# Attention and FFN layer: output projection as three fp32r passes, normalisation in PSUM, query rounded by ScalarE

## The reference

```
xn   = layernorm(x)
q    = xn @ Wq + bq                      16 heads of 16
k, v = ctx @ Wk + bk, ctx @ Wv + bv      one head, shared by all
attn = softmax(mask(q k^T / 4)) v        64 keys
x    = x + attn @ Wo + bo
h    = layernorm(x)
m    = mix0 * h[t-1] + mix1 * h[t] + mix2 * h[t+1]
s    = tanh(m @ Wo1 + bo1) @ Wo2 + bo2   a score for each of 9 paths
p    = argmax(s)
c    = (m @ W1[p] + b1[p]) @ W2[p] + b2[p]
out  = x + layernorm(h + c) * gamma + beta
```

## Time and profile before

| what | value |
|---|---|
| median of three runs | 359.27 us (357.69 to 359.3) |
| the profiled execution's own time | 357.65 us |
| its span | 355.8 us |
| PE busy | 312.0 us, 88% |
| DVE busy | 282.4 us, 79% |
| POOL busy | 188.2 us, 53% |
| ACT busy | 183.0 us, 51% |
| mean granted clock of PE | 0.973 of full speed |
| `project_out`'s matmuls (L584) | 128 records, mean 390 ns, 31.3 us |

### The profile page before, as it was taken

One profiled execution on the slowest core, in us unless ns is written; L12 is line 12 of the kernel. 1 busy time (PEld: TensorE's weight loads), 2 busy tenths in 40 slices (PEclk: granted clock), 3 DMA queues, 4 the chain that ended last, 5 costly groups with the idle time before them and its releaser, 6 DMA issues.

```text
span 355.8 us, 7313 instructions
## 1 busy us (share of the span) xinstructions
PE 312.0 (88%) x2700; PEld 230.7 (65%) x2700; DVE 282.4 (79%) x606; ACT 183.0 (51%) x285; POOL 188.2 (53%) x226
## 2 busy tenths in 40 slices
PE   1588788765999999999999999999999999799990
PEld 1374364452667957795678767876678568677980
DVE  2675398595769899889989898989798866689866
ACT  1452835625764477537851777258444752367400
POOL 0444002633178179944895299728881787164044
PEclk9998999996999999999999999999999999899996
DMA  7509500020002001200110010000100010001003
GB/s 210 177 0 218 106 0 1 2 76 0 0 4 76 0 2 62 73 3 0 59 52 22 0 59 0 0 0 2 61 0 2 2 61 2 0 0 62 3 0 118
DMA packets 20564, 13.44 MB, mean 38 GB/s; under 512 B 10097, under 2 KB 20282, under 8 KB 20538
## 3 DMA queue, kind: packets, MB, share of 16 engines
q1 hardware_dynamic: 18898, 12.53, 12.0%
q10 hardware_dynamic: 1640, 0.57, 0.7%
HBM read 8.90 MB, written 4.19 MB: 37 GB/s over the span
## 4 chain that ended last, share of the span: by engine, by line
PE 76%; DVE 12%; ACT 5%; issue 3%; POOL 2%; DMA 1%; DVEq 0%; ACTq 0%; POOLq 0%
PE ps L429 16%; PE ps L434 7%; PE ps L584 7%; PE ps L668 6%; PE ps L673 5%; PE ps L669 5%; PE ps L541 5%; PE ps L566 4%; PE ps L560 4%; DVE mx L1115 3%; DVE osb L1139 3%; PE ps L650 2%; PE ps L544 2%; PE ps L635 2%; PE ps L481 2%
## 5 line engine op out<-in xcount | busy, mean ns | idle before, releaser
L1408 POOL TENSOR_TENSOR rs<-ve,halfneg 128x4 f32<-128x4 f32 x24 | 26.7, 1113 | 106.8 <-DVE ve L1078 106.8
L843 ACT ACTIVATE e<-ps 128x1024 f32<-128x1024 f32 x32 | 31.1, 1024 | 20.3 <-PE ps L548 20.3
L1115 DVE TENSOR_REDUCE mx<-ps 128x16 f32<-128x1024 f32 x32 | 37.9, 1216 | 0.3 <-PE ps L516 0.3
L668 PE MATMUL ps<-w2h,hmh 128*128 128x256 f32 (+1 forms) x140 | 35.6, 288 | 0.0
L669 PE MATMUL ps<-w2l,hmh 128*128 128x256 f32 (+1 forms) x140 | 34.7, 283 | 0.0
L1465 POOL TENSOR_TENSOR hml<-hs,hmh 128x512 fp32r<-128x512 f32 x24 | 30.3, 1276 | 7.4 <-ACT hmh L904 7.3
L868 ACT ACTIVATE xh<-x,vb,rs 128x256 f32<-128x256 f32 x32 | 16.6, 591 | 33.5 <-POOL vb L1421 33.5
L584 PE MATMUL ps<-wo,osb 128*128 128x256 f32 x128 | 31.3, 390 | 2.0 <-DVE osb L1139 2.0
L894 ACT ACTIVATE hs<-ps,b1s 128x512 f32<-128x512 f32 x28 | 19.3, 689 | 24.4 <-PE ps L434 24.4
L1454 POOL TENSOR_TENSOR y<-xh2f,gms 128x256 f32<-128x256 f32 x28 | 22.2, 824 | 17.5 <-DVE xh2f L1087 17.5
L429 PE MATMUL ps<-xmh,w1h 128*128 128x512 f32 x80 | 27.8, 429 | 3.3 <-DVE xmh L1190 3.3
(11 more groups left out here) (161 smaller groups left out, 787.5 us busy)
## 6 DMA issues: line engine op xcount, KB each, us to landing
xin<-in_x SPq DMA_DIRECT2D x8, 512.0 KB, 4.1
out<-y SPq DMA_DIRECT2D x7, 512.0 KB, 2.9
min_<-in_mask_Bx1xSxS_ik SPq DMA_DIRECT2D x8, 128.0 KB, 4.8
hs<-in_L_ffn_W SPq DMA_DIRECT2D x2, 288.0 KB
y<-in_constants SPq DMA_DIRECT2D x1, 512.0 KB, 8.7
hs<-in_L_ffn_W SPq DMA_DIRECT2D x1, 512.0 KB
out<-xin SPq DMA_DIRECT2D x2, 256.0 KB, 2.2
cst<-in_constants SPq DMA_DIRECT2D x1, 384.0 KB, 6.0
```

The source lines that it names most:

```text
L668: nc.tensor.matmul(o, L.hi(m, r)[:, ks], w2h[0:r, m, :], start=(m == 0), stop=False)
L843: nc.scalar.activation(e[:, 2 * i:2 * i + 2, :], ps[:, bank:bank + 2, :], ACT.Exp).then_inc(s_e, 1)
L1115: v.tensor_reduce(mx[:, k, :].rearrange("p (a h) -> p a h", a=2), ps[:, bank:bank + 2, :].rearrange("p a (h s) -> p a h s", s=SK), AX.X, A ...
L1408: g.tensor_tensor(ln[7][:, :], ln[6][:, :], halfneg[:, :], ALU.pow).then_inc(s_r, 1)
```

## The change

Wo is split once into a rounded part `woh` (ACT) and a remainder `wol` (POOL), and PE's wait before the first step with an n is for `wol`. Wo is loaded into the memory of `osb`. The normalised attention output is no longer written back to `osb`: DVE multiplies in two halves of 256 tokens (both groups c together, 512 columns) into the same PSUM banks 4 and 5, which are laid out by halves now; ACT rounds each half from PSUM to `osh` (`attn_hi`), DVE subtracts to `osl` (`attn_lo`); these use the memory of `xTh` and `xTl`. A pair of tiles of the projection is 12 fp32r matmuls. In a step with all parts the order of PE, DVE and ACT changes as shown. The query's rounding moves there from DVE to one copy on ACT. The scratch of `argmax` moves to PSUM, and the read of the gate's bank is signalled at its last reduction. `wk8` moves into memory of `e`.

```diff
@@ PE
             def project_out(b, j, tiles):
                 if tiles[0] == 0:
                     pe.wait_ge(s_osb, at(b, NJ, j + 1))
+                    pe.wait_ge(s_osl, at(b, NJ, j + 1))
+                else:
                     pe.wait_ge(s_oT, at(b, NJ, j + 1))
                 for k in tiles:
+                    o, ks = ps[:, k // 2, (k % 2) * D:(k % 2 + 1) * D], slice(k * P, (k + 1) * P)
+                    two_pass_out(o, ks)
                     for c in range(KD):
-                        mm = nc.tensor.matmul(ps[:, k // 2, (k % 2) * D:(k % 2 + 1) * D], osb[:, c, k * P:(k + 1) * P],
-                                              wo[:, c, :], start=(c == 0), stop=(c == KD - 1))
+                        mm = nc.tensor.matmul(o, osl[:, c, ks], woh[:, c, :], start=False, stop=(c == KD - 1))
                 mm.then_inc(s_wo, 1)
+            def two_pass_out(o, ks):
+                for c in range(KD):
+                    nc.tensor.matmul(o, osh[:, c, ks], woh[:, c, :], start=(c == 0), stop=False)
+                    nc.tensor.matmul(o, osh[:, c, ks], wol[:, c, :], start=False, stop=False)
@@ PE step, from rep 2 on
                     rep(*f, 2)
+                    project_out(*n, (0, 1))
+                    rep(*f, 3)
                     if front:
                         scores_for_max(*front, 1, banks)
-                elif front:
-                    scores_for_max(*front, 2, banks)
-                    scores_for_max(*front, 3, banks)
-                if n:
-                    project_out(*n, (0, 1))
-                if f:
-                    rep(*f, 3)
+                    project_out(*n, (2, 3))
+                    rep(*f, 4)
+                    w2_tiles(*f, (0, 1))
                     if front:
                         scores_for_max(*front, 2, banks)
-                    rep(*f, 4)
-                if n:
-                    project_out(*n, (2, 3))
-                if f and front:
-                    scores_for_max(*front, 3, banks)
-                if f:
-                    w2_tiles(*f, (0, 1))
-                    w2_tiles(*f, (2, 3))
+                    w2_tiles(*f, (2,))
+                    if front:
+                        scores_for_max(*front, 3, banks)
+                    w2_tiles(*f, (3,))
+                else:
+                    if front:
+                        scores_for_max(*front, 2, banks)
+                        scores_for_max(*front, 3, banks)
+                    if n:
+                        project_out(*n, (0, 1))
+                        project_out(*n, (2, 3))
@@ PE, before the first step with an n
-            pe.wait_ge(s_wo_in, 32)
+            pe.wait_ge(s_wol, 1)
@@ ACT
+            def q_round(b, j):
+                act.wait_ge(s_q, at(b, NJ * KD, (j + 1) * KD))
+                nc.scalar.activation(qr[:, :, :], q[:, :, :], ACT.Copy).then_inc(s_qr, 1)
+            def attn_hi(b, j, half):
+                act.wait_ge(s_nrm, at(b, 2 * NJ, 2 * j + half + 1))
+                t = slice(half * CH // 2, (half + 1) * CH // 2)
+                nc.scalar.activation(osh[:, :, t], spread_half(half), ACT.Copy).then_inc(s_osh, 1)
@@ ACT step
+                if front and f:
+                    q_round(*front)
                 if n:
                     pv_copy(*n)
                 if f:
                     hidden(*f, 2)
                     hidden(*f, 3)
+                    selected_hi(*f, 0)
+                    attn_hi(*n, 0)
+                    attn_hi(*n, 1)
+                    for m in range(1, NM):
+                        selected_hi(*f, m)
                     keep_xh2(*f)
-                    for m in range(NM):
-                        selected_hi(*f, m)
...
+                if n and not f:
+                    attn_hi(*n, 0)
+                    attn_hi(*n, 1)
@@ ACT, after the step without an n
+            act.wait_ge(s_wo_in, 32)
+            nc.scalar.activation(woh[:, :, :], wo32, ACT.Copy).then_inc(s_woh, 1)
@@ DVE
             def attn_normalise(b, j):
                 dve.wait_ge(s_bc, at(b, NJ, j + 1))
                 dve.wait_ge(s_osb, at(b, NJ, j + 1))
-                v.tensor_tensor(osb[:, :, :], osb[:, :, :], ps[:, 4:6, :], ALU.mult).then_inc(s_oT, 1)
+                for half in range(2):
+                    t = slice(half * CH // 2, (half + 1) * CH // 2)
+                    v.tensor_tensor(spread_half(half), osb[:, :, t], spread_half(half), ALU.mult).then_inc(s_nrm, 1)
+            def attn_lo(b, j, front):
+                if front:
+                    dve.wait_ge(s_qp, at(b, NJ * KD, (j + 2) * KD))
+                for half in range(2):
+                    dve.wait_ge(s_osh, at(b, 2 * NJ, 2 * j + half + 1))
+                    t = slice(half * CH // 2, (half + 1) * CH // 2)
+                    v.tensor_tensor(osl[:, :, t], spread_half(half), osh[:, :, t].bitcast(F32),
+                                    ALU.subtract).then_inc((s_osl, s_oT)[half], 1)
@@ DVE step
-                if front:
+                if front and not f:
                     q_round(*front)
...
                     attn_normalise(*n)
                 if f:
                     select(*f, 1)
+                if n:
+                    attn_lo(*n, front)
+                if f:
                     select(*f, 2)
-                    if front:
-                        take_max(*front, 0, banks)
-                        take_max(*front, 1, banks)
                     select(*f, 3)
                     select(*f, 4)
+                    x1_stats(*n, 0)
+                    x1_stats(*n, 1)
                     if front:
-                        take_max(*front, 2, banks)
-                    if n:
-                        x1_stats(*n, 0)
-                        x1_stats(*n, 1)
-                    if front:
-                        take_max(*front, 3, banks)
+                        for k in range(NT):
+                            take_max(*front, k, banks)
                         split_max(*front)
@@ POOL, after the step without an n
+            pool.wait_ge(s_woh, 1)
+            g.tensor_tensor(wol[:, :, :], wo32, woh[:, :, :].bitcast(F32), ALU.subtract).then_inc(s_wol, 1)
```

More of the change, by code:

```diff
@@ L115, in layer_program @@
         w2h, w2l = sb("w2h", [P, NM, D], F32R), sb("w2l", [P, NM, D], F32R)
-        wo = sb("wo", [P, KD, D])
+        woh, wol = sb("woh", [P, KD, D], F32R), sb("wol", [P, KD, D], F32R)
         wo2 = sb("wo2", [P, NPATH])
         wk = sb("wk", [P, KD, DK])
-        wk8 = sb("wk8", [P, KD, P])
         wv = sb("wv", [P, KD, DK])
@@ L160, in layer_program @@
         ctx_in = e[0:SK, 0:2, :].rearrange("p a (b d) -> p (a b) d", d=D)
+        wk8 = e[:, 4, 0:KD * P].rearrange("p (c n) -> p c n", c=KD)
         ctxT = e[:, 2:4, :].rearrange("p c (b a s) -> p c b a s", b=B, a=2)
@@ L165, in layer_program @@
         osb = sb("osb", [P, KD, CH])
+        wo32 = osb[:, :, 0:D]
+        osh, osl = xTh, xTl
         x1 = sb("x1", [P, NJ, NT, D])
@@ L235, in layer_program @@
         s_inv, s_invh = sem("denominators_inverted"), sem("inverse_rounded")
-        s_rd, s_bc, s_oT = sem("inverse_split"), sem("inverse_spread"), sem("attn_normalised")
+        s_rd, s_bc = sem("inverse_split"), sem("inverse_spread")
+        s_nrm, s_osh, s_osl, s_oT = sem("attn_normalised"), sem("attn_hi"), sem("attn_lo_first_half"), sem("attn_lo")
+        s_woh, s_wol = sem("wo_hi"), sem("wo_lo")
         s_wo, s_x1 = sem("wo_in_psum"), sem("x1_done")
@@ L243, in layer_program @@
         s_f, s_fa, s_fv = sem("ffn_slot_filled"), sem("ffn_slot_read_by_act"), sem("ffn_slot_read_by_dve")
-        s_gmax, s_gcand, s_gidx, s_oh = sem("gate_max"), sem("gate_cand"), sem("gate_index"), sem("onehot")
+        s_gsum, s_gmax, s_gcand, s_oh = sem("gate_sum"), sem("gate_max"), sem("gate_cand"), sem("onehot")
         s_x1b, s_yg, s_yo = sem("x1_plus_beta"), sem("times_gamma"), sem("out_ready")
@@ L258, in layer_program, with spread_half @@
         mr = mask.rearrange("b o (j k p) s -> p (b o) j k s", p=P, k=NT)
+        def spread_half(half):
+            return ps[:, 4 + half, :].rearrange("p (c t) -> p c t", c=KD)
         def quarter(g):
@@ L401, in _ @@
             load(bos[:, :], row_broadcast(bo, D), s_wo_in)
-            load(wo[:, :, :], Wo.rearrange("(c p) n -> p c n", p=P), s_wo_in)
+            load(wo32, Wo.rearrange("(c p) n -> p c n", p=P), s_wo_in)
             next_inputs(0, 0)
@@ L846, in pv_copy @@
                 act.wait_ge(s_o, at(b, NJ, j + 1))
-                act.wait_ge(s_wo, at(b, 2 * NJ, 2 * j))
+                act.wait_ge(s_nrm, at(b, 2 * NJ, 2 * j))
+                act.wait_ge(s_wol, 1)
                 nc.scalar.activation(osb[:, :, :], ps[:, 0:2, :], ACT.Copy).then_inc(s_osb, 1)
+            def attn_hi(b, j, half):
+                act.wait_ge(s_nrm, at(b, 2 * NJ, 2 * j + half + 1))
+                t = slice(half * CH // 2, (half + 1) * CH // 2)
+                nc.scalar.activation(osh[:, :, t], spread_half(half), ACT.Copy).then_inc(s_osh, 1)
```

(20 more changed lines are left out.)

4 lines of the change are left out of this document (1 added, 3 removed).

## The result

The changed kernel takes **385.19 us** (median of 4 runs, 383.82 to 386.34) against 358.48 us (354.67 to 359.3) for the kernel before: ratio 1.0757, 95% interval [1.0718, 1.0796]. Forecast were 376 us and a range of 360 to 386. The profiled execution took 386.34 us with a span of 384.5, 28.7 us more than the 355.8 of before. Executions at a lower granted clock that took over 1.5% longer than the fastest of their kernel (there are some in experiments 6 and 9) are left out of its time and ratio.

What follows compares the result with a forecast made beforehand. TensorE (PE) was taken as the loop's bound. To 357.65 us were added 12.5 (five full steps), 2.6 (A's start), 0.85 (A's end), 1.45 (B) and 1.0 (C, the step without front): +18.4, 376 us; range 360 to 386.

Steps and rivals of the forecast that it cites:

- The five idle times: PE's waits in a full step: before projection 1.4, first w2 tile 1.1, score tile 2 0.85, maxima's transposition 0.3 us.
- the first w2 tile: Full step: PE waits 1.1 us for selection 4's rounding on ACT and remainder on POOL.
- score tile 2: Full step: PE waits 0.85 us until DVE's first maximum frees the banks.
- the first wait: Full step, before the projection: PE waits 1.4 us, until 223.5, for DVE's first subtraction.
- the forecast alone: The prediction's main case without its rivals: +13 to +23 us, 371 to 381 us, chance 57%.
- A full step: One of five steps with attention, next scores and earlier FFN: +2.5 us each, five times +12.5.
- A's start: First of two steps without FFN: PE waits for Wo's remainder before it, +2.6 us (0 to 3.0).
- A's and B's end: Ends of the two steps without FFN: DVE's extra 1.45 us delays the maxima, +0.85 in A, +1.45 in B.
- PE stays the bound: Rival: projection inputs arrive in time, each chunk saves 0.96 us, whole 350 us; chance 11%.
- Only the first wait counts: Rival: w2 tiles and maxima find inputs ready, full step about +0.5 us, whole 366 us; chance 20%.
- The clock falls in the full steps: Rival: new stalls lower PE's clock, 1.8 us of work lost per full step, +9, 385 us; chance 6%.
- the row at 68 us: Profile before, 68 to 70 us: full clock with PE working 0.67 of 2 us, cited against a clock loss.

Runs made afterwards that it cites:

- experiment 6: Changed kernel with the earlier kernel's order in full steps (score tiles ahead of projection and w2, maxima between selections): 376.25 us, ratio 1.0485.
- experiment 9: Kernel of experiment 8 with denominators ahead of P·V, spread before last w1 tile, subtractions around selections 0 and 1, half of GpSimd's additions later: 365.5 us, ratio 1.0176.
- Experiment 3: Changed kernel without the attention output's remainder (no third pass, no DVE subtractions): 364.79 us, ratio 1.0195.
- experiment 7: Kernel of experiment 6 with 16 spare matmuls on constants filling PE's 1.93 us wait: 371.6 us, ratio 1.0333.
- experiment 10: Kernel of experiment 9 with the denominators behind P·V again in the first two steps (no FFN): 362.94 us, ratio 1.0126.
- experiment 1: Kernel before, with 12 fp32r matmuls per projection pair, all from rounded operands, no remainders and no new wait: 353.89 us, ratio 0.989.
- experiment 2: Changed kernel without PE's wait for Wo's remainder ahead of the first step with attention: 382.75 us, ratio 1.065.
- experiment 4: Kernel before, with only q's rounding on ACT in full steps and the argmax scratch in PSUM: 359.5 us, ratio 1.0009.
- experiment 5: Changed kernel with both subtractions ahead of selection 1 on DVE: 379.74 us, ratio 1.0598.
- experiment 8: Changed kernel, spread in banks 0 and 1, projection, selections and maxima reordered, no early wait for Wo's remainder: 366.05 us, ratio 1.0214.

## Why the prediction was right, and where it was short

*The order of events was right.* Counted from the turn of the step, the kernel after runs 20.93 us behind the one before, and on that scale the projection begins at 223.56 (predicted 223.5), `rep` 4 ends at 227.96 (227.63), selection 4 starts at 228.07 (227.7), the transposition of the maxima at 238.91 (238.2). The five idle times and their releasers are those named; only the first w2 tile waited less than forecast (0.30 and 0.38, not 1.1), because PE reached it later, and score tile 2 less (0.57, not 0.85) for the same reason. Experiment 3 shows that the first wait hangs on the subtraction: without it 0.17 us are left of the 1.42.

*The range held by luck.* 385.19 lies outside the 371 to 381 that the forecast alone covers, and 0.8 us under the upper end of the range. That end was left open for a dearer product into PSUM, and the product was not dearer: 0.69 us for a half, with 0.68 assumed. By the ends that the prediction names, with its +7 for the product and 3.0 instead of 2.6 for the start, the sum would reach only 383.4. Sign and mechanism were earned; that the range reached the result was not.

*A full step: +3.2, not +2.5.* The waits sum to 2.87 us (3.65 predicted, with 0.2 of small waits to go). Two terms of PE's own work were mis-sized. Its saving: 12 x 0.12 = 1.44 for a pair was taken from the inside of a w2 tile, but the pair measures 1.58, so the two pairs of a step fall from 3.85 to 3.15, by 0.70 and not 0.96. And the w2 tiles, whose own time the prediction left as it was: from the first row to the transposition of the maxima, waits and score tiles taken out, they hold PE for 8.40 us (248.89 to 259.84, less 1.45 and 1.10), against 7.28 before (228.42 to 235.70), where nothing parts them. The rows show why. In an unbroken row a matmul starts 0.12 us behind the one before it; ahead of a wait the last one runs out its 0.28 (249.82 to 250.10), and the first one behind a wait or a score tile takes 0.39, the next starting 0.22 behind it (250.40 to 250.62). 2.87 less 0.70 plus 1.12 is 3.3; the rest of the step is 0.1 shorter. The other kernels separate this term: in experiments 6 and 7, with w2 in one piece, the four tiles take 7.3 us as before, and in experiments 9 and 10, without waits of 0.2 us but with a score tile between, 7.8 to 7.9 (some 0.3 of it, in experiment 10, is small gaps among the first tile's remainders). That uses up nearly all that the projection saves there, and so their step is 37.7 and not the 37.15 of experiment 1. A kernel with the inputs early and w2 in one piece was not run.

*A's start: +3.02 for 2.6*, the mechanism as named; the wait ends with GpSimd's remainder. *A's and B's end:* B +1.36 for 1.45. In A, the part from the second group of transposed scores on (42.54 us) is 18.72 us against 17.79 in the kernel before, +0.93 for 0.85. Its other 1.34 us lie ahead of that, where PE works at half clock for longer (0.50 until 41 us; before, until some 32.5). That term was left out; but most of it does not come from the 2.73 us of standing. This part takes 7.75 us in the changed kernel and 6.41 before, 7.43 in experiment 2, without the standing, 7.47 in experiment 4, where the projection is as before, and 7.1 to 7.2 in experiments 3, 5 and 6, with the standing.

*Two sums that do not go with the projection.* The 3.15 us before A: the pairs of Wq's matmuls at 18 to 23 us take 1.05 instead of 0.62. The kernel of experiment 4, with no word of the projection changed, has them at 1.05 too (transposition at 30.94), that of experiment 3 at 0.62 (28.20). One row of each, after and experiment 4:

```profile
18.82 1.06 PE L436 MATMUL ps<-xTh,wql 128*128 128x512 f32 x2
...
18.33 1.05 PE L429 MATMUL ps<-xTh,wql 128*128 128x512 f32 x2
```

Each kernel has one profile, so no trace shows that it comes and goes between executions of one kernel; but the four executions of experiment 4 range from 356.17 to 361.46, and the profiled one is the slowest. I take it as some 3 us of noise on one profile, of which the medians (26.7 us apart) should carry less than the profiles (28.7). And of the first full step's +4.71, 1.57 are ahead of its second group of transposed scores, at half clock (8.71 us to there against 7.14); experiment 9 has 8.75 there, all the others 7.1 to 7.2, behind a stand of 4.0 to 5.3 us in every one of them.

*The rivals.* "PE stays the bound" (350) needed the inputs in time; experiment 1 is that case, and would have given 353.9. "Only the first wait counts" (366) is refuted by the rows at 250.40 to 254.50. "The clock falls in the full steps" (385) came out at the right time for a wrong reason: in the profile the granted clock of the loop stayed at 1.00 through waits of 1.42 us and less. But the row at 68 us, by which the prediction set this rival aside, was weaker than it looked. At the same place of the changed kernel, in B, PE stands for 1.52 us, and the granted clock behind it is 0.55:

```profile
77.59 0.39 PE L519 MATMUL ps<-cst,mT 64*128 64x512 bf16 x2 [1.52 <-DVE rDs L1170]
```

```profile
80.00:86.00 6.00, 5.54 (x33) 5.06 (x30) 5.79 (x9) 1.19 (x2) 1.72 (x3) 0.55 0.36 108
```

Ten of the twelve kernels have this stand, of 1.51 to 1.53 us. In five the clock falls to 0.50 soon behind it (the changed one and experiments 1, 3, 4 and 7), in five it stays at 1.00 (the one before and experiments 2, 5, 6 and 8). Experiment 6, with its waiting in one piece of 1.93 us, loses the clock in three of five full steps, and experiment 7 in none. So what a stand of 1.5 to 1.9 us does to the clock is not told by its length. The rule of the Trainium skill that the prediction weighed ("TensorE: Matmul & The Clock Gate", Part 1: The HAM clock gate: throttled by default, released by activity) agrees with experiments 6 and 7, 0.50 in three steps with the wait idle and 1.00 in all with it filled.

*Left open:* why equal stands keep the clock in one step and lose it in another; what decides how long it stays low after the 4.0 to 5.3 us of standing at the end of B, and in the first matmuls of the program.

## What to carry to other kernels

When PE's queue is the bound, a cheaper matmul is worth what PE saves only if its operands need no operation more than before: here 0.57 us a step were bought with a chain of three operations, of which two had nowhere to hide. Ask first which buffer forces the chain into its place; moving the spread to other banks and the additions behind the remainders gave back most of it. Count what a new order does to PE's unbroken rows as well: each cut in them costs time that no idle column shows. An idle stretch can also cost the clock behind it, and filling it with spare matmuls gave that back where it had. The first steps of a pipeline, where less runs beside, need an order of their own.

## What the runs showed of the hardware

- A DVE product with one input and its result in PSUM, in place, takes 0.69 us for 512 columns, like the one that writes SBUF (0.68); the argmax's operations on 36 columns take 0.20 us each with their scratch in PSUM.
- A stand of PE of 1.93 us between busy stretches lowered the granted clock to 0.50 for 3 to 4 us in three of five steps of one execution and left it at 1.00 in the other two; one of 1.51 to 1.53 us was followed by 0.50 in five of ten kernels. Stands of 1.42, 0.30, 0.38 and 0.57 us in one step did not.
- Sixteen matmuls whose result nobody reads made a kernel 4.7 us faster.
- Parting the four w2 tiles by waits and score tiles made PE's own time for them 8.40 us instead of 7.28.
- Pairs of matmuls at 18 to 23 us ran at 1.05 instead of 0.62, throughout or in part, in nine of the twelve profiles, while the profile's granted clock there says 1.00 in eight of them.
